# A three-block hybrid (Mamba scan, minGRU, ternary FFN) in one kernel: rows of C by DMA, fewer two-input reads from SBUF on VectorE, new slots

## The reference, cut to what matters

```
# a: Mamba block
h = layernorm(x); xi, z = split(h @ W_in)                 # 2 x 256
u = silu(causal_conv4(xi) + b_conv)
dt_r, B, C = split(u @ W_x)                               # 8, 16, 16
dt = softplus(dt_r @ W_dt + b_dt); A = -exp(A_log)        # 256 x 16
for s in tokens: state = exp(dt*A) * state + (dt*u) (x) B; y = state . C
x = x + ((y + u*Dskip) * silu(z)) @ W_out
# FFN with ternary weights (twice: after a, and at the end), norm and gelu around it
w_t = sign(w) * (|w| > 0.5*mean|w|)                       # up 128->512, down 512->128
# b: minGRU
x_in, x_skip = silu(x@W1+b1), silu(x@W2+b2)               # 512 each
z = sigmoid(x_in@Wz+bz); g = x_in@Wh+bh
h_s = (1-z) * h_(s-1) + z * g                             # scan along tokens
x = (x_skip + h) @ Wo + bo                                # plus the residual
```

## Time and profile before

| | |
|---|---|
| median of 3 timed runs | 898.15 us (897.51 to 898.35) |
| the profiled execution | 889.54 us |
| its span | 887.7 us |
| first state scan starts | 43.94 us |
| last state scan starts | 770.74 us |

### The profile page before, as it was taken

One profiled execution on the slowest core, in us unless ns is written; L12 is line 12 of the kernel. 1 busy time (PEld: TensorE's weight loads), 2 busy tenths in 40 slices (PEclk: granted clock), 3 DMA queues, 4 the chain that ended last, 5 costly groups with the idle time before them and its releaser, 6 DMA issues.

```text
span 887.7 us, 12333 instructions
## 1 busy us (share of the span) xinstructions
PE 710.7 (80%) x4058; PEld 592.8 (67%) x4058; DVE 704.4 (79%) x965; ACT 628.4 (71%) x944; POOL 593.0 (67%) x374
## 2 busy tenths in 40 slices
PE   2353665669979996999779987999799968897975
PEld 2143454558867785778767876778677857786774
DVE  2489987889989999799979997999799997844241
ACT  4764666678788968897789779787889487526313
POOL 3178956866787869776968687777968567515312
PEclk9575856889979999899989997999899997998996
DMA  2441111111111112121111211121112111000000
GB/s 46 111 163 51 65 57 59 48 49 48 61 45 41 61 39 57 41 67 50 49 49 43 66 48 48 41 69 40 45 49 60 49 31 40 13 1 1 13 1 13
DMA packets 35185, 42.79 MB, mean 48 GB/s; under 512 B 7457, under 2 KB 17074, under 8 KB 35122
## 3 DMA queue, kind: packets, MB, share of 16 engines
q1 hardware_dynamic: 35122, 42.00, 15.5%
HBM read 39.63 MB, written 2.36 MB: 47 GB/s over the span
## 4 chain that ended last, share of the span: by engine, by line
PE 44%; DVE 24%; issue 12%; POOL 10%; ACT 9%; DMA 0%; DVEq 0%; ACTq 0%; POOLq 0%
DVE state L923 10%; PE work L1110 7%; PE work L1112 7%; PE work L1111 7%; PE y_ps L1203 5%; PE work L1252 4%; DVE state L930 3%; POOL inflow L380 3%; POOL in_lo L535 3%; PE y_ps L1186 2%; PE c_ps L1194 2%; PE work L1239 2%; POOL wide L526 2%; ACT dA L701 1%; PE work L1221 1%
## 5 line engine op out<-in xcount | busy, mean ns | idle before, releaser
L380 POOL TENSOR_TENSOR inflow<-dtu,b_all 128x1024 f32<-128x1024 f32 x127 | 311.7, 2457 | 119.0 <-DVE state L923 85.8
L923 DVE TENSOR_TENSOR_SCAN state<-dA,inflow 128x1024 f32<-128x1024 f32 x128 | 292.4, 2285 | 18.7 <-ACT dA L701 16.1
L1203 PE MATMUL y_ps<-ident,state 128*128 128x128 f32 x1024 | 152.5, 298 | 30.5 <-DVE state L930 30.5
L930 DVE TENSOR_TENSOR state<-state,c_ps 128x1024 f32<-128x1024 f32 x128 | 155.5, 1215 | 20.9 <-PE c_ps L1194 19.7
L1203 PEld LDWEIGHTS y_ps<-ident,state 128*128 128x128 f32 x1024 | 134.9, 156 | 47.1 <-DVE state L930 36.3
L700 ACT ACTIVATE dA<-dt,decay_c 128x512 f32<-128x512 f32 x128 | 88.0, 688 | 94.5 <-DVE state L923 90.0
L1110 PE MATMUL work<-in_hi,wzh_hi 128*128 128x512 f32 x256 | 105.4, 412 | 4.6 <-POOL in_lo L535 4.5
L1112 PE MATMUL work<-in_lo,wzh_hi 128*128 128x512 f32 x256 | 101.1, 395 | 0.0
L1111 PE MATMUL work<-in_hi,wzh_lo 128*128 128x512 f32 x256 | 100.9, 394 | 0.0
L701 ACT ACTIVATE dA<-dt,decay_c 128x511 f32<-128x511 f32 x128 | 86.2, 673 | 0.0
L1194 PE MATMUL c_ps<-xd,pick 128*128 128x512 f32 x128 | 62.8, 491 | 25.0 <-DVE state L930 24.4
(11 more groups left out here) (163 smaller groups left out, 1562.0 us busy)
## 6 DMA issues: line engine op xcount, KB each, us to landing
b_all<-b_scratch SPq DMA_DIRECT2D x128, 256.0 KB, 3.1
x_tok<-in_x SPq DMA_DIRECT2D x8, 256.0 KB, 3.8
out_x<-x_tok SPq DMA_DIRECT2D x8, 256.0 KB, 3.7
wide<-in_Wz SPq DMA_DIRECT2D x1, 1024.0 KB, 7.3
wide<-in_Wh SPq DMA_DIRECT2D x1, 1024.0 KB, 9.5
skip_f<-in_W SPq DMA_DIRECT2D x2, 256.0 KB, 5.4
dtu<-in_W_in SPq DMA_DIRECT2D x1, 256.0 KB
b_scratch<-gated SPq DMA_DIRECT2D x8, 32.0 KB, 1.8
```

Source lines behind the costliest of these rows:

```text
L380: eng.tensor_tensor(inflow[:, n % 2, :, :], dtu[:, :, :], b_all[:, n % RING, :].unsqueeze(1).broadcast_to([P, HALVES, SEQ]), ALU.mult).the ...
L923: dve.tensor_tensor_scan(flat(state[:, g % 3, :, :]), flat(dA[:, :, :]), flat(inflow[:, n % 2, :, :]), 0.0, ALU.mult, ALU.add).then_inc(s_ ...
L930: dve.tensor_tensor(state[:, g % 3, :, :], state[:, g % 3, :, :], c_ps[:, :].unsqueeze(1).broadcast_to([P, HALVES, SEQ]), ALU.mult).then_i ...
L1203: last = pe.matmul(y_region(j, h), state[:, g % 3, h, cols(j)], ident[:, :], is_transpose=True, start=False, stop=(n == STATE - 1), skip_g ...
```

## The change

In words:

- `c_ps`, `pick` and the 128 matmuls L1194 go. C is written to the DRAM scratch with B (32 rows in place of 16), and SP loads its rows into `c_all` (ring of 2) as it does for B (ring of 3, was 4). The read multiplies state by `c_all`, so both operands lie in SBUF. The freed PSUM bank becomes a fourth `work` bank. xd no longer has two buffers.
- `in_hi` is written by ACT, as a second Silu of the same bank, in place of DVE's cast.
- The gate stays tanh; the second ACT operation goes. W_h is halved once, on ACT, in row 0; `new` is (tanh + 1) * bank, in place in PSUM, and `keep` is 0.5 - 0.5*tanh.
- bh isn't added to each token. The scan runs on h - bh, starting from -bh (`nbh_c`), and bh @ Wo is added to bo once (`bias_out`). The GRU scan reads keep from SBUF and the candidate from PSUM.
- Operations on 4 or 8 columns on DVE (eps, means, scales) change from TENSOR_SCALAR and SCALAR_TENSOR_TENSOR to TENSOR_TENSOR with constant tiles (nine memsets more).
- All slots and banks are new, with exceptions for rows 0, 6 and 7. The code can cut a row into pieces (`UNITS`), but the eight units are the eight whole rows.

```diff
-RING = 4
+B_RING, C_RING = 3, 2
-BANKS = 3
+BANKS = 4
...
+            def c_load(b, n):
+                g = STATE * b + n
+                wait(sp, s_read, g - C_RING + 1)
+                sp.dma_start(c_all[:, g % C_RING, tok(b)], bc_dram[b % 2, STATE + n, tok(b)].partition_broadcast(P)
+                             ).then_inc(s_cring[g % C_RING], 16)
...
+            for b in range(N):
+                for n in range(STATE):
+                    if n + B_RING < STATE:
+                        b_load(b, n + B_RING)
+                    elif b + 1 < N:
+                        if n + B_RING == STATE:
+                            b_store(b + 1)
+                        b_load(b + 1, n + B_RING - STATE)
+                    if n + C_RING < STATE:
+                        c_load(b, n + C_RING)
+                    elif b + 1 < N:
+                        c_load(b + 1, n + C_RING - STATE)
+                    if n == 1 and b + 2 < N:
+                        load_x(b + 2)
...
             def round_wzh(k):
+                act.activation(wzh_f[:, k, FF:2 * FF], wzh_f[:, k, FF:2 * FF], ACT.Copy, scale=0.5).then_inc(s_halved, 1)
...
-                    act.activation(in_f[:, j, :], bank(p)[:, :], ACT.Silu, bias=b1_c[:, j:j + 1]
+                    act.activation(in_f[:, j, tok(t)], bank(p)[:, tok(t)], ACT.Silu, bias=b1_c[:, j:j + 1])
+                    act.activation(in_hi[:, j, tok(t)], bank(p)[:, tok(t)], ACT.Silu, bias=b1_c[:, j:j + 1]
                                    ).then_inc(*emptied(p))
...
-                act.activation(gate[:, j % 2, :], gate[:, j % 2, :], ACT.Copy, scale=0.5, bias=0.5).then_inc(s_gate1, 1)
...
-                dve.tensor_scalar(m_vv[:, 0, :], m_mv[:, :, 1], LN_EPS, None, ALU.add)
-                dve.tensor_scalar(m_vv[:, 1, :], m_mv[:, :, 1], 1.0 + LN_EPS, LN_EPS * LN_EPS, ALU.mult, ALU.add
-                                  ).then_inc(s_mvv, 1)
+                dve.tensor_tensor(m_away[:, tl(b)], m_mv[:, tl(b), 0], minus_one[:, tl(b)], ALU.mult)
+                var = m_mv[:, tl(b), 1].unsqueeze(1).broadcast_to([P, 2, len(tiles(b))])
+                dve.tensor_tensor(m_vv[:, :, tl(b)], var, m_grow[:, :, tl(b)], ALU.mult).then_inc(s_mgrow, 1)
+                dve.wait_ge(s_mgrow, b + 1)
+                dve.tensor_tensor(m_vv[:, :, tl(b)], m_vv[:, :, tl(b)], m_eps[:, :, tl(b)], ALU.add).then_inc(s_mvv, 1)
...
             def mix_read(b, n):
                 g = STATE * b + n
                 dve.wait_ge(s_scan, g + 1)
-                dve.wait_ge(s_cps, g + 1)
-                dve.tensor_tensor(state[:, g % 3, :, :], state[:, g % 3, :, :],
-                                  c_ps[:, :].unsqueeze(1).broadcast_to([P, HALVES, SEQ]), ALU.mult
+                dve.wait_ge(s_cring[g % C_RING], 16 * (g // C_RING + 1))
+                dve.tensor_tensor(state[:, g % 3, :, tok(b)], state[:, g % 3, :, tok(b)],
+                                  c_all[:, g % C_RING, tok(b)].unsqueeze(1).broadcast_to([P, HALVES, TO[b] - FROM[b]]), ALU.mult
                                   ).then_inc(s_read, 1)
...
-            def gru_in_hi(t, j, r, s):
-                dve.tensor_copy(in_hi[:, j, :], in_f[:, j, :]).then_inc(s_inhi, 1)
...
+                dve.scalar_tensor_tensor(bank(p)[:, tok(t)], gate[:, j % 2, tok(t)], 1.0, bank(p)[:, tok(t)],
+                                         ALU.add, ALU.mult).then_inc(s_new, 1)
...
-                dve.tensor_tensor_scan(mixed[:, j, :], keep[:, j % 2, :], mixed[:, j, :], 0.0,
-                                       ALU.mult, ALU.add).then_inc(s_hid, 1)
+                first = nbh_c[:, j:j + 1] if FROM[t] == 0 else mixed[:, j, FROM[t] - 1:FROM[t]]
+                dve.tensor_tensor_scan(mixed[:, j, tok(t)], keep[:, j % 2, tok(t)], bank(p)[:, tok(t)], first,
+                                       ALU.mult, ALU.add).then_inc(*emptied(p))
...
-            def mix_cn(b, n):
-                if n == 0:
-                    evacuated(pe, b, "xdbl")
-                wait(pe, s_read, STATE * b + n)
-                pe.matmul(c_ps[:, :], pick[:, n:n + 1].broadcast_to([P, P]), xd[:, b % 2, :], start=True, stop=True
-                          ).then_inc(s_cps, 1)
...
+            def bias_out():
+                pe.wait_ge(s_abs, 2)
+                bank_free(0, "bo")
+                for k in range(FB):
+                    last = pe.matmul(bank("bo")[:, 0:D], bh_c[:, k:k + 1].broadcast_to([P, P]), wo_sb[:, k, :],
+                                     start=(k == 0), stop=(k == FB - 1))
+                last.then_inc(*made("bo"))
```

More of the change, by code:

```diff
@@ L144, in times, with has @@
+START = [unit[3] for unit in UNITS]
+STEP = [(end - first) / SEQ for _, first, end, _ in UNITS]
 def times(eng, at):
-    return {op: [STATE * b + MOVED.get((eng, op, b), at[op]) for b in range(ROWS)] for op in at}
+    return {op: [START[b] + MOVED.get((eng, op, b), at[op]) for b in range(N)] for op in at}
+def has(p, b):
+    return {"zin0": FROM[b] < SEQ // 2, "zin1": TO[b] > SEQ // 2}.get(p, b == 0 or p not in ONCE)
 POOL_ON, ACT_ON, DVE_ON, PE_ON = (times("POOL", POOL_AT), times("ACT", ACT_AT), times("DVE", DVE_AT),
@@ L158, in due @@
 def due(r, s, on, n=0):
-    return [b for b in range(ROWS) if on[b] + n == STATE * r + s]
+    return [b for b in range(N) if on[b] + n * STEP[b] == STATE * r + s]
 def latest(r, s, on):
@@ L179, with mark, tok, tl @@
 MARK = {pb: i + 1 for k in range(BANKS) for i, pb in enumerate(SEQUENCE[k])}
+def mark(p, b):
+    p = p.split("+")[0]
+    while b >= 0 and (p, b) not in MARK:
+        b -= 1
+    return MARK[p, b] if b >= 0 else 0
+def tok(b):
+    return slice(FROM[b], TO[b])
+def tl(b):
+    return slice(FROM[b] // P, TO[b] // P)
+def tiles(b):
+    return range(FROM[b] // P, TO[b] // P)
 def build(nc, x, gamma, beta, W_in, W_conv, b_conv, W_x, W_dt, b_dt, A_log, Dskip, W_out,
@@ L722, in norm_hi @@
                 full(act, t, "norm%d" % m)
-                act.activation(n_hi[:, :], bank("norm%d" % m)[:, :], ACT.Copy).then_inc(s_nhi[m], 1)
+                act.activation(n_hi[:, tok(t)], bank("norm%d" % m)[:, tok(t)], ACT.Copy).then_inc(s_nhi[m], 1)
             def ffn_gelu(t, c, j, r, s):
@@ L752, in gru_in @@
                     act.wait_ge(s_lo12, 1)
-                    act.activation(skip_f[:, j - FB, :], bank(p)[:, :], ACT.Silu, bias=b2_c[:, j - FB:j - FB + 1]
+                    act.activation(skip_f[:, j - FB, tok(t)], bank(p)[:, tok(t)], ACT.Silu, bias=b2_c[:, j - FB:j - FB + 1]
                                    ).then_inc(*emptied(p))
@@ L857, in ternary_thresholds @@
                 evacuated(dve, 0, "abs")
+            def bias_out():
+                full(dve, 0, "bo")
+                dve.tensor_tensor(bo_tok[:, :], bo_tok[:, :], bank("bo")[:, 0:D], ALU.add).then_inc(*emptied("bo"))
             def ternary_signs(k):
@@ L922, in mix_scan, with carried @@
                 wait(dve, s_acc, g - 2)
-                dve.tensor_tensor_scan(flat(state[:, g % 3, :, :]), flat(dA[:, :, :]), flat(inflow[:, n % 2, :, :]),
-                                       0.0, ALU.mult, ALU.add).then_inc(s_scan, 1)
+                if TO[b] - FROM[b] == SEQ:
+                    dve.tensor_tensor_scan(flat(state[:, g % 3, :, :]), flat(dA[:, :, :]),
+                                           flat(inflow[:, n % 2, :, :]), 0.0, ALU.mult, ALU.add).then_inc(s_scan, 1)
+                else:
+                    for h in range(HALVES):
+                        first = 0.0 if FROM[b] == 0 else carry[:, n, h:h + 1]
+                        last = dve.tensor_tensor_scan(state[:, g % 3, h, tok(b)], dA[:, h, tok(b)],
+                                                      inflow[:, n % 2, h, tok(b)], first, ALU.mult, ALU.add)
+                    last.then_inc(s_scan, 1)
+                    if TO[b] < SEQ:
+                        dve.wait_ge(s_scan, g + 1)
+                        dve.tensor_tensor(carry[:, n, :], state[:, g % 3, :, TO[b] - 1], one[:, 0:HALVES], ALU.mult).then_inc(s_carry, 1)
+            def carried(b, n):
+                return n + 1 + STATE * sum(TO[k] < SEQ for k in range(b)) if TO[b] < SEQ else 0
             def mix_read(b, n):
@@ L1141, in mix_in @@
                 bank_free(b, p)
-                three(bank(p)[:, :], win_hi[:, cols(h)], win_lo[:, cols(h)], h_hi[:, :], h_lo[:, :]
+                seen = slice(max(FROM[b] - TAPS, 0), TO[b])
+                three(bank(p)[:, seen], win_hi[:, cols(h)], win_lo[:, cols(h)], h_hi[:, seen], h_lo[:, seen]
                       ).then_inc(*made(p))
@@ L1161, in mix_xdbl @@
                 for h in range(HALVES):
-                    last = pe.matmul(bank("xdbl")[:, :], wx_rep[:, h, :], u[:, h, :], start=(h == 0),
+                    last = pe.matmul(bank("xdbl")[:, tok(b)], wx_rep[:, h, :], u[:, h, tok(b)], start=(h == 0),
                                      stop=(h == HALVES - 1))
@@ L1182, in mix_skip @@
                 pe.wait_ge(s_diag, 1)
-                wait(pe, s_gtok, 2 * b)
```

(17 more changed lines are left out.)

440 lines of the change are left out of this document (235 added, 205 removed), and 115 rows, old and new, of tables (ACT_AT, BANK, DVE_AT, MOVED).

## The result

The changed kernel takes **960.6 us** (median of 4 runs, 957.5 to 961.9) against 897.8 before (4 runs): ratio 1.070, interval 1.067 to 1.073. The forecast was 893 us and its range ended at 930. The profiled execution of before, 889.5 us, was a quick one, 8 us under its median, so a difference read from the two profiles is up to 9 us larger than the 63 us between the medians.

A forecast was written before the change was run, and what follows sets the result against it. Rows with a scan were taken as paced by DVE and PE together, the tail by PE. DVE net +21 (75 added, 54 removed), -24 absorbed, +2 loads, -4 bank, slots, PE and ACT: -5 on 898.15, 893 us; range 845 to 930.

The forecast's parts named there:

- Turns of the multiply: DVE's 128 reads with C in SBUF wait for POOL instructions in flight, as the scan does: 75 us added on DVE.
- A: Rival: the reads' multiply does not take turns with POOL; DVE saves 68 us, time 851 us; chance 0.27.
- I take half, 4 us in each of six full rows, 24.: DVE's other idle spells, near 8 us a row, absorb half as port waits let ACT and PE catch up: 24 us.
- B: The forecast itself: reads take turns with POOL, mean near 1.8 us, maximum past 3; 893 us, chance 0.38.
- C, turns feed on themselves: Rival: reads also hold up POOL, 80 us in all; read waits 106 us instead of 75; 924 us, chance 0.33.
- threshold of 80 us: Total read waits deciding the outcome, 54 + 24 + 4 - 2; below 80 us waited the kernel is faster.
- Removed from DVE before 774 us: 25.9 + 12.: DVE loses 32 casts, 25.9 us, and GRU scans gain 12 us with one operand in PSUM.
- 83%, not the limit: ACT, with second Silus replacing copies, ends 2.4 us lighter a row; at 83% it isn't the limit.
- Small operations: DVE's 4-column operations become TENSOR_TENSOR, one more per norm: 2.9 us; nothing returns if the new form takes turns.
- -4 for bank and slots: Fourth work bank, new slots, and lighter PE and ACT: -4 us, from -10 to +6.
- c_ps, loads, the rest: DVE's 19.0 us of waits for c_ps go; row 0's loads, behind Wz and Wh, add 2 us.
- D: Rival: C rows land late, 9.6 us mid-kernel; reads wait 525 us in all, over 1400 us; chance 0.02.

The follow-up runs named there:

- the SBUF read: Kernel before with only each state's read multiplying by a constant SBUF tile instead of c_ps in PSUM; c_ps still formed and waited for: 978.5 us, 1.091.
- C by DMA: Kernel before with C's rows loaded by DMA, read from SBUF, no c_ps products; old slots, banks, GRU and small operations: 960.7 us, 1.073.
- small forms: Kernel before with only the norms' operations on 4 or 8 columns written as TENSOR_TENSOR with constants in SBUF: 903.4 us, 1.008.
- GRU part: Kernel before with tanh gate, halved candidate weights, bias outside the scan and in_hi by a second Silu on ACT; candidate in SBUF, old slots: 901.6 us, 1.006.
- measured together: Kernel before with C loaded by DMA, TENSOR_TENSOR small operations and the GRU changes, but old slots, three banks and candidate in SBUF: 972.5 us, 1.086.
- even DVE load: Kernel before with an extra DVE copy of c_ps into an unused tile ahead of each read, no turns with POOL: 939.0 us, 1.049.
- Fixed delays on both engines: Kernel before with DVE fillers at eight reads of a row and POOL fillers before inflows and other operations, as lengths held up earlier: 953.2 us, 1.063.

## Why the prediction was wrong

The parts add up, in us against before, from the runs: the SBUF read +82; c_ps gone -18 (C by DMA +64); small forms +7; GRU part +5 (sum 76, measured together +77); slots, bank and PSUM candidate -14. Total +63.

*Turns of the multiply.* Right: it takes turns as the scan does. A, at 0.27, is excluded. The overlay gave 75 us of rests (what is left of a POOL instruction when a read begins) for before's timeline; reads alone lost 72, in the changed kernel 61. So this term was sized well, with some luck: with the SBUF read the rests grew to 92 us, and only 71 of them were waited for, since not every POOL instruction holds a read up (see the last section).

*"I take half, 4 us in each of six full rows, 24."* This step failed. An even DVE load is absorbed by half (88 us cost 43), but a wait for the port is no such load. It comes when both engines have work, and whatever starts on POOL beneath the read slips too: +103 us, for which the forecast B had no term. Per us of wait the read cost 1.1; the forecast's own price was 51 for 75, or 0.7. Where 51 was booked 82 was due: 31 us. Fixed delays on both engines reproduced 56 of the 82; why it is 82 stays open in part.

*C, turns feed on themselves.* The nearest. Its "+80 us" on POOL was +72 in the changed kernel, its 84 us of POOL in a row were 81 to 85 (74.1 in the earlier trace rows). But its reason for a loss, 106 us of waits, did not come. Its threshold of 80 us waited at the reads was wrong, since it rested on the 54 removed and the 24 absorbed: 61 were enough.

*"Removed from DVE before 774 us: 25.9 + 12."* This step failed by as much. I counted the casts' 25.9 us in full and kept ACT out as "83%, not the limit". Alone the GRU part, with the candidate still in SBUF, costs 5 us: 31 off. A share of 83% says nothing about the moment: the second Silus stand right ahead of the dA that the next scan needs. The 12 us of the scans were in no run by themselves; in the changed kernel they fell to 1.26 us, near the 1.21 that I booked, and count below with the bank.

*Small operations.* "+2.9, nothing returns": in place +7. In the changed kernel they took 55 us more by their new neighbours on POOL, in either form. What they cost there is not told apart; with slots, bank and candidate they net -14, where I had booked -16: -4 for bank and slots (PE and ACT included) and -12 for the candidate's scans. That this came out near is partly luck, since 40 us of waits that I had not seen are inside it.

*c_ps, loads, the rest.* 19 us of waits gone, less 2 for row 0's loads: 18 measured. D: C lands in 3.3 us, no wait. So of the 68 us between -5 and +63 the reads' price makes 31, the casts 31 and the small forms 4; c_ps and slots together make about 1. ACT has 12 or 13 table loads in a middle row, not 11. PE's clock did fall, from 0.96 to between 0.90 and 0.94 in the middle rows, where I expected no fall: PE was busy 82 to 85 us in each of them, not 80 (84.0 before). Sign by sign: mean 1.70 with a maximum of 3.43 was B's, the period of 101 to 107 C's. inflow's median did not rise (2.37), which B and C both had said; its mean did, from 2.46 to 2.70, since 81 of the 127 inflows are untouched (under 2.45 us).

## What to carry to other kernels

Where DVE and POOL share a loop, keep one operand of each DVE tensor-tensor operation in PSUM, even at the price of a matmul and a wait: here 128 operands moved to SBUF cost 64 us, although 20 us of waits for the matmul went with them. Price such a wait on both engines, since the same collisions delay POOL too (here by 103 us, DVE's reads by 72); an absorption that holds for an even load need not hold for it. And count an engine's relief only after asking what the engine that takes the work has queued behind it.

## What the hardware showed that I had not expected

A POOL instruction does not hold the pair for its whole length in every case. Reads begun beside POOL's powers over 8 columns (root and m_root, 1.65 us long) were not delayed. In the changed kernel there were nine, with 10 us of those instructions still to run by their records, all at 1.21 to 1.23 us, and eight of the nine powers kept their length too. This is one of the reads, beside the root at 347.31 above:

```profile
347.75 1.22 DVE L1043 TENSOR_TENSOR state<-state,c_all 128x1024 f32<-128x1024 f32 x1
```

The Trainium skill, on the page named above, has the pair taken "for the whole instruction"; for these powers the trace differs, and the measurement decides.

The start of an instruction in the timeline doesn't prove that it has the pair, either. In the kernel with the SBUF read five reads began 0.02 to 0.11 us after a base_tok (128x128) and took 1.22 us. There POOL was the one that waited: that base_tok took 1.49 us against 0.45 alone. These are three of them in a row, in the kernel with the SBUF read and in the kernel before, each with a read begun beside the second:

```profile
385.91 2.36 POOL L502 TENSOR_SCALAR base_tok<-x_tok,m_gain,m_shift 128x128 f32<-128x128 f32 x3
```

```profile
347.15 1.31 POOL L502 TENSOR_SCALAR base_tok<-x_tok,m_gain,m_shift 128x128 f32<-128x128 f32 x3
```

And operations of four columns with a single SBUF input wait like those with two: TENSOR_SCALAR 0.84 us in the mean, TENSOR_TENSOR in the same place 0.84. The prediction had read from L880 that they wait; new is how much it can come to.
